# Probabilities of three slots in eight turned by a transposing DMA; q and k written and read in two steps

## Chip, core and metric

One core of a Trainium2 chip runs the kernel. The metric is the device time of one execution in microseconds. Engines are TensorE (PE, with PEld for its weight loads), VectorE (DVE), ScalarE (ACT), GpSimd (POOL) and the DMA queues, which SP, ACT and POOL issue.

## What is computed

```python
xn = layernorm(x)                                  # x: 8 x 512 x 256
qkv = (xn @ qkv_w.T).reshape(8, 512, 3, H=16, D=64)
q, k = rope(q), rope(k)
scores = einsum('bhqd,bhkd->bhqk', q, k) / 8
kb = -p * log1p(a * |i - j|)                       # p, a: one number a head
attn = softmax(scores + kb)
att = einsum('bhqk,bhkd->bhqd', attn, v) -> @ out_w.T
out = x + att + ffn(xn)                            # ffn: top-1 routing over 16 experts
```

Between q, k and the output, each head of each batch has 512 x 512 probabilities. They are made with queries on the partitions and are wanted, for the product with v, with keys on the partitions: they have to be turned, in blocks of 128 x 128.

## The kernel before

`prepare` and `experts` run first (layer norm, routing, weights, the 16 experts). They are not touched. `attention` is the rest, and the change lies in it alone.

**Slots and groups.** The attention is cut into 256 slots, 32 for each of 8 batches. Slot s takes one *pair*: two of the four 128-row query blocks of one head, 2 x 128 queries by 512 keys. Eight slots make a group, that is four heads of one batch; there are 32 groups. Each of the engines has its own hand-written program, and they are held together by semaphores alone. What stands in each engine's slot s:

- PE (`slot` at its end of the file): scores of s into `ps_s[0]` and `ps_s[1]` (four matmuls, L1296 and L1297; it waits until the scores of s-1 have been read, `negated`); a *fill*, one piece of other work in the single bank `ps_x` (q or k of the group after next in slots 0 to 3 of the group, v in slots 4 and 5, the output projection y of the group before in 6 and 7; it waits for `x_free`); eight transposes of pair s-1 into `ps_t` (L1307); the values, 24 matmuls of pair s-2 (L1323).
- DVE: `neg` of s (L1207, once for each of the two query blocks: scaled scores plus bias, negated, with the row minimum); the read of a v or y fill; `pair_lo` of s-1 (L1172), which subtracts the f16 high part of the turned probabilities from `ps_t`; in every fourth slot `read_context` ahead of neg, in the next `context_lo` at the end (L1193).
- ACT: the read of a q, k or v fill; `pair_hi` of s-1 (L1087), the f16 high part out of `ps_t`; the two exponentials of s (L1111), out of `neg` into `prob`.
- POOL: `step`, the rotation of q and k of one group (L998 to L1002) and their split into high and low f16 parts `parts` (L1008, L1012); then the gathers and sums of the expert outputs.
- SP: `turn_context`, a transposing DMA of the context's f16 parts into `ot` (L958); `move`, which writes `parts` to DRAM in four DMAs (L945), waits for them, and reads them back as `qk` and `kswap` in three (L949, L951).

All operands of large matmuls are f16 pairs, high and low part, so a product takes three matmuls (`PARTS`). Buffers `prob`, `pt`, `ps_t` and `neg` are double, by the slot's parity; `ps_s` has one bank for each query block.

## Time and profile before

| | us |
|---|---|
| median of 3 runs | 1342.48 (1341.34 to 1347.08) |
| profiled execution, device time | 1339.31 |
| its span | 1337.5 |
| attention, from its first scores to the end | about 359 to 1337 |
| one group of eight slots in the middle | 30.09 |

The page's second section shows the stages: up to about 340 us preparation and experts, with changing loads on all engines; from there an even pattern, in which PE is in nines, DVE in eights, ACT in sevens and eights. The engines' spans overlap, so a busy share tells only where to look. Which engine holds the others up is read from the waits, and what a slot costs from the chain of work in order of time: there, each piece is the time from one instruction's release to the next one's. Matmul records overlap, so their mean durations (193 ns for 64 columns) are not their cost; the chain's pieces are.

### The profile page before, as it was taken

The numbers are of one execution on the slowest core, as the hardware profiler recorded it, in microseconds if no ns is written. First come the engines' busy times: TensorE is split into PE (matmuls) and PEld (weight loads), VectorE is DVE, ScalarE is ACT, GpSimd is POOL, SyncE is SP. The second block draws the span as 40 slices with busy tenths as digits, with TensorE's granted clock in tenths as the row PEclk, the third lists the DMA queues.
The fourth block names the chain that finished last, engine by engine and source line by source line (L and its number), as shares of the span: only waits on it lengthen the run. The fifth ranks groups of instructions, "written<-read, shape, count | busy, mean of one in ns | idle before, by whom it ended". The sixth has DMA issues, their size and how long they took to land.

```text
span 1337.5 us, 33943 instructions
## 1 busy us (share of the span) xinstructions
PE 1216.2 (91%) x13412; PEld 938.0 (70%) x13412; DVE 1098.9 (82%) x2166; ACT 985.9 (74%) x1831; POOL 798.0 (60%) x628
## 2 busy tenths in 40 slices
PE   5630999997699999999999999999999999999995
PEld 5620788895267777777777777777777777777764
DVE  7864799994388888888888888888888888888894
ACT  2775688882388777777778777877778777877773
POOL 3044000001788887886788788877778887886600
PEclk9975899998899999999999999999999999999998
DMA  8625666661445444444553454355445444444411
GB/s 267 237 62 187 219 236 234 234 212 40 117 123 141 104 111 127 120 117 115 147 154 98 112 151 104 96 141 142 117 130 146 105 112 127 120 118 113 135 41 48
DMA packets 172685, 182.47 MB, mean 136 GB/s; under 512 B 78066, under 2 KB 150783, under 8 KB 172528
## 3 DMA queue, kind: packets, MB, share of 16 engines
q1 hardware_dynamic: 160256, 160.03, 41.9%
q0 software_dynamic: 4352, 12.41, 2.7%
q10 hardware_dynamic: 7920, 7.87, 2.0%
q8 instruction: 106, 1.74, 0.5%
q14 instruction: 51, 0.42, 0.1%
HBM read 109.12 MB, written 54.56 MB: 122 GB/s over the span
## 4 chain that ended last, share of the span: by engine, by line
PE 71%; ACT 1%; DMA 1%; issue 1%; DVE 1%; SPq 0%; ACTq 0%; DVEq 0%
PE ps_t L1307 17%; PE ps_o L1323 13%; PE ps_x L1263 13%; PE ps_s L1296 8%; PE ps_s L1297 8%; PE ps_x L1283 7%; PE ps_x L1273 6%; ACT prob L1111 1%; DMA kswap<-qk_dram 0%; DMA qk_dram<-parts 0%; DMA ot<-ctx_parts 0%; ACT proj L1073 0%; ACT prob L1073 0%; DVE ctx_parts L1193 0%; ACT pt_hi L1087 0%
## 5 line engine op out<-in xcount | busy, mean ns | idle before, releaser
L1172 DVE SCALAR_TENSOR_TENSOR pt_lo<-ps_t,pt_hi 128x1024 f16<-128x1024 f32 x256 | 312.6, 1221 | 129.1 <-ACT pt_hi L1087 129.1
L1207 DVE CUSTOM_DVE_ANT_0 neg<-ps_s,strips,score_scale 128x512 f32<-128x512 f32 x512 | 361.7, 743 | 8.1 <-PE ps_s L1297 8.0
L1111 ACT ACTIVATE prob<-neg,neg_max 128x512 f32<-128x512 f32 x512 | 362.6, 712 | 0.0
L1087 ACT ACTIVATE pt_hi<-ps_t 128x1024 f16<-128x1024 f32 x256 | 261.9, 1023 | 128.5 <-PE ps_t L1307 126.5
L1307 PE MATMUL ps_t<-ident,prob 128*128 128x128 f32 x2048 | 269.4, 273 | 4.3 <-ACT prob L1111 4.2
L1307 PEld LDWEIGHTS ps_t<-ident,prob 128*128 128x128 f32 x2048 | 234.3, 141 | 39.1 <-issue 10.6
L1323 PE MATMUL ps_o<-val_hi,pt_hi 128*128 128x64 f16 x2048 | 206.0, 193 | 1.8 <-DVE pt_lo L1172 1.7
L1323 PE MATMUL ps_o<-val_hi,pt_lo 128*128 128x64 f16 x2048 | 206.2, 193 | 0.0
L1323 PE MATMUL ps_o<-val_lo,pt_hi 128*128 128x64 f16 x2048 | 206.2, 193 | 0.0
L1296 PE MATMUL ps_s<-qk 128*128 128x512 f16 x512 | 195.4, 382 | 6.0 <-DMA kswap<-qk_dram 5.6
L1297 PE MATMUL ps_s<-kswap,qk 128*128 128x512 f16 x512 | 194.9, 381 | 0.0
L1323 PEld LDWEIGHTS ps_o<-val_hi,pt_hi 128*128 128x128 f16 x2048 | 184.4, 98 | 2.6 <-DVE pt_lo L1172 1.8
L1323 PEld LDWEIGHTS ps_o<-val_lo,pt_hi 128*128 128x128 f16 x2048 | 181.7, 98 | 2.9
L1323 PEld LDWEIGHTS ps_o<-val_hi,pt_lo 128*128 128x128 f16 x2048 | 181.9, 98 | 0.0
L998 POOL TENSOR_TENSOR rot<-proj,cos 128x512 f32<-128x512 f32 x62 | 78.7, 1269 | 164.5 <-ACT proj L1073 151.6
L1002 POOL TENSOR_TENSOR rot<-rot,prod 128x512 f32<-128x512 f32 x124 | 168.1, 1355 | 9.7
L1263 PE MATMUL ps_x<-xcur,wqkv_hi 128*128 128x512 f16 x512 | 154.2, 383 | 10.9 <-PEq L533 6.1
L1012 POOL TENSOR_TENSOR parts<-rot,parts 128x1024 f16<-128x1024 f32 x62 | 132.5, 2138 | 4.8
L624 POOL DMA_DIRECT2D expert_dram<-xa x16 | 11.5, 721 | 177.2 <-ACT xa L665 177.2
L1073 ACT COPY proj<-ps_x 128x512 f32<-128x512 f32 x124 | 73.0, 589 | 49.3 <-PE ps_x L1263 49.3
L1283 PE MATMUL ps_x<-wout_hi,ot 128*128 128x256 f16 x512 | 97.1, 278 | 7.0 <-DMA ot<-ctx_parts 6.1
L1263 PEld LDWEIGHTS ps_x<-xcur,wqkv_hi 128*128 128x128 f16 x512 | 49.8, 99 | 74.6 <-issue 8.5
(186 smaller groups left out, 2565.0 us busy)
## 6 DMA issues: line engine op xcount, KB each, us to landing
raw<-in_L_ffn_w_dram SPq DMA_DIRECT2D x32, 1024.0 KB, 5.1
qk_dram<-parts SPq DMA_DIRECT2D x128, 256.0 KB
qk<-qk_dram SPq DMA_DIRECT2D x32, 1024.0 KB, 5.6
kswap<-qk_dram SPq DMA_DIRECT2D x64, 256.0 KB, 6.5
xa<-in_L_attn_x_dram SPq DMA_DIRECT2D x8, 512.0 KB, 6.4
xt_dram<-xth SPq DMA_DIRECT2D x8, 512.0 KB, 5.1
slots_dram<-zeros SPq DMA_DIRECT2D x4, 1024.0 KB, 8.3
xa<-slots_dram SPq DMA_DIRECT2D x16, 256.0 KB, 5.3
```

The costliest lines, as they stand in the source:

```text
L1002: nc.gpsimd.tensor_tensor(rot[:, w, half, :], rot[:, w, half, :], prod[:], op).then_inc(turned_parts, 1)
L1012: nc.gpsimd.tensor_tensor(parts[:, w, 1], rot[:, w], parts[:, w, 0], ALU.subtract).then_inc(parts_lo, 1)
L1087: nc.scalar.activation(pt[0][:, (l - 1) % 2].rearrange("p q k c -> p q (k c)"), ps_t[l % 2][:], ACT.Copy, scale=P_SCALE).then_inc(turned_h ...
L1111: nc.scalar.activation(prob[:, l % 2, q, :], neg[:, l % 2, q, :], ACT.Exp, bias=neg_max[:, 2 * (l % 2) + q:2 * (l % 2) + q + 1], scale=-1. ...
L1172: nc.vector.scalar_tensor_tensor(out=pt[1][:, (l - 1) % 2].rearrange("p q k c -> p q (k c)"), in0=ps_t[l % 2][:], scalar=P_SCALE, in1=pt[0 ...
L1207: nc.vector.tensor_tensor_reduce(neg[:, l % 2, q, :], ps_s[q][:], strips[:, h, start:start + S], score_scale[:, 0:1], 3.0e38, ALU.add, ALU ...
L1263: last = nc.tensor.matmul(ps_x[:], wt[a][:, kt, c:c + P], xcur[:, x, kt, :], start=(m == 0), stop=(m == 3 * KT - 1))
L1283: last = nc.tensor.matmul(ps_x[:, i * M:(i + 1) * M], ot[:, x, kt, t:t + P], wot[a][:, 2 * g + kt, :], start=(m == 0), stop=(m == 5))
L1296: nc.tensor.matmul(ps_s[q][:], qk[:, j % 2, 0, k // 2, t:t + P], qk[:, j % 2, 1, k // 2, :], start=True, stop=False)
L1297: nc.tensor.matmul(ps_s[q][:], qk[:, j % 2, 0, k // 2, t:t + P], kswap[:, j % 2, k // 2, :], start=False, stop=True).then_inc(scored, 1)
L1307: last = nc.tensor.transpose(ps_t[l % 2][:, q, kt * P:(kt + 1) * P], prob[:, (l - 1) % 2, q, kt * P:(kt + 1) * P], ident[:])
L1323: last = nc.tensor.matmul(ps_o[:, c:c + D], pt[x][:, l % 2, q, kt, :], val[a][:, l2 // 8 % 4, kt, hd:hd + D], start=(m == 0), stop=(m == 3 ...
```

## The change

In slots 1, 4 and 7 of each group (`DMA_TURNS`, 95 of the 256 pairs, since the last pair stays with PE) the pair isn't transposed by PE. ACT makes the f16 high part of the unturned probabilities behind the exponentials (`prob_high`), DVE the low part at the head of its next slot (`prob_low`), both into a single buffer `prob_parts`, and SP turns both parts with one DMA straight into `pt` (`turn_probs`). PE's values wait for that DMA. `pt` is now one tile with the parts inside.

SP's `move` is cut in two: `move_out` writes q and k at a group's end, `move_in` reads them in the next group, behind the turn of the last pair. `rot` has room for q or k only, so the high and low parts of q are made before k is rotated.

```diff
 EARLY_SCATTERS = 24
+DMA_TURNS = (1, 4, 7)
 FILLS = 6
...
-        rot = sb("rot", [P, 2, 2, S])
+        rot = sb("rot", [P, 2, S])
...
-        pt = [sb(f"pt_{n}", [P, 2, 2, TPB, P], F16) for n in ("hi", "lo")]
+        pt = sb("pt", [P, 2, 2, 2, TPB, P], F16)
+        prob_parts = sb("prob_parts", [P, 2, 2, S], F16)
...
             return n
-        def pairs_turned(b, l):
-            return PAIRS * b + l
+        def by_dma(s):
+            return s % 8 in DMA_TURNS and s < NB * PAIRS - 1
+        def dma_slots(s):
+            return sum(by_dma(i) for i in range(s))
+        def pe_slots(s):
+            return s - dma_slots(s)
         def y_fills(b, j):
...
         @block.sync
         def _(sp):
-            def move(n, r):
+            def move_out(n, r):
                 F = 2 * n + r
-                wait(sp, scored, 16 * (F - 1))
                 sp.wait_ge(parts_lo, 2 * F + 2)
                 for h in range(HG):
                     sp.dma_start(qk_dram[r, :, :, :, :, h, :].rearrange("w a f d s -> d (w a f) s"),
                                  parts[32 * h:32 * h + 32].rearrange("p w a f s -> p (w a f) s")).then_inc(parts_written, 16)
+            def move_in(n, r):
+                F = 2 * n + r
+                wait(sp, scored, 16 * (F - 1))
                 sp.wait_ge(parts_written, 64 * F + 64)
                 rows = qk_dram[r].rearrange("w a f d h s -> (a f d) w (h s)")
                 sp.dma_start(qk[:, r].rearrange("p w h s -> p w (h s)"), rows).then_inc(qk_moved[r], 16)
                 for c in (0, 64):
                     sp.dma_start(kswap[64 - c:128 - c, r].rearrange("p h s -> p (h s)"), rows[c:c + 64, 1]).then_inc(qk_moved[r], 16)
+            def turn_probs(s):
+                n = dma_slots(s)
+                wait(sp, pv_done, s - 1)
+                sp.wait_ge(prob_lo, n + 1)
+                sp.dma_start_transpose(pt[:, s % 2].rearrange("p a q k c -> p (a q k) c"),
+                                       prob_parts[:].rearrange("p a q s -> p (a q s)")).then_inc(turned_by_dma, 16)
             def turn_context(b, j):
...
                 sp.dma_start(source[:], source_dram[b]).then_inc(routes_loaded, 16)
                 sp.dma_start(gate[:], gate_dram[b]).then_inc(routes_loaded, 16)
-            def batch(b):
+            def group(b, j):
+                first = PAIRS * b + 8 * j
+                if first and by_dma(first - 1):
+                    turn_probs(first - 1)
+                if first + 8 < NB * PAIRS:
+                    move_in((4 * b + j + 1) // 2, (j + 1) % 2)
+                for k in range(7):
+                    if by_dma(first + k):
+                        turn_probs(first + k)
+                    if k == 1 and first:
+                        turn_context(*divmod(4 * b + j - 1, 4))
+                    if k == 1 and j == 1 and not is_last(b):
+                        load_routes(b + 1)
+                if ahead(b, j):
+                    move_out(*ahead(b, j)[:2])
+                if j == 1 and not is_last(b):
+                    sp.wait_ge(filled, fills_before(b, 14))
+                    load_x(b + 1)
+            load_routes(0)
+            move_out(0, 0)
+            move_in(0, 0)
+            move_out(0, 1)
+            for b in range(NB):
                 for j in range(4):
-                    if j or not is_first(b):
-                        turn_context(b, j - 1)
-                    if j == 1 and not is_last(b):
-                        load_routes(b + 1)
-                        sp.wait_ge(filled, fills_before(b, 14))
-                        load_x(b + 1)
-                    if ahead(b, j):
-                        move(*ahead(b, j)[:2])
-            load_routes(0)
-            move(0, 0)
-            move(0, 1)
-            over_batches(batch)
+                    group(b, j)
             turn_context(NB - 1, 3)
             sp.wait_ge(x_free, fills_before(NB - 1, PAIRS) + 2)
...
                 for half, (first, second, op) in enumerate(((cos, sin, ALU.subtract), (sin, cos, ALU.add))):
-                    nc.gpsimd.tensor_tensor(rot[:, w, half, :], proj[:, w, 0, :], first[:], ALU.mult).then_inc(turned_parts, 1)
+                    nc.gpsimd.tensor_tensor(rot[:, half, :], proj[:, w, 0, :], first[:], ALU.mult).then_inc(turned_parts, 1)
...
             def high(F, w):
-                nc.gpsimd.tensor_copy(parts[:, w, 0], rot[:, w]).then_inc(parts_hi, 1)
+                nc.gpsimd.tensor_copy(parts[:, w, 0], rot[:]).then_inc(parts_hi, 1)
             def low(F, w):
-                nc.gpsimd.tensor_tensor(parts[:, w, 1], rot[:, w], parts[:, w, 0], ALU.subtract).then_inc(parts_lo, 1)
+                nc.gpsimd.tensor_tensor(parts[:, w, 1], rot[:], parts[:, w, 0], ALU.subtract).then_inc(parts_lo, 1)
             def step(F, fills):
                 for w in range(2):
                     rotate(F, w, fills + 2 * w + 2)
-                for w in range(2):
                     if F > 1:
                         high(F, w)
...
             def pair_hi(b, l):
-                act.wait_ge(turned, pairs_turned(b, l))
-                wait(act, pv_done, PAIRS * b + l - 2)
-                nc.scalar.activation(pt[0][:, (l - 1) % 2].rearrange("p q k c -> p q (k c)"), ps_t[l % 2][:],
+                s = PAIRS * b + l - 1
+                act.wait_ge(turned, pe_slots(s) + 1)
+                wait(act, pv_done, s - 1)
+                nc.scalar.activation(pt[:, s % 2, 0].rearrange("p q k c -> p q (k c)"), ps_t[l % 2][:],
                                      ACT.Copy, scale=P_SCALE).then_inc(turned_hi, 1)
+            def prob_high(s):
+                n = dma_slots(s)
+                act.wait_ge(exp_done, 2 * s + 2)
+                wait(act, turned_by_dma, 16 * n)
+                nc.scalar.activation(prob_parts[:, 0], prob[:, s % 2], ACT.Copy, scale=P_SCALE).then_inc(prob_hi, 1)
             def context_hi(b, l):
...
+                if s and not by_dma(s - 1):
                     pair_hi(b, l)
                 for q in range(2):
                     act.wait_ge(negated, 2 * s + q + 1)
-                    if q == 0:
-                        wait(act, turned, pairs_turned(b, l - 1))
+                    if q == 0 and s >= 2:
+                        if by_dma(s - 2):
+                            act.wait_ge(prob_lo, dma_slots(s - 1))
+                        else:
+                            act.wait_ge(turned, pe_slots(s - 1))
                     nc.scalar.activation(prob[:, l % 2, q, :], neg[:, l % 2, q, :], ACT.Exp,
                                          bias=neg_max[:, 2 * (l % 2) + q:2 * (l % 2) + q + 1], scale=-1.0,
                                          accum_out=sums[:, l // 4 % 2, 2 * (l % 4) + q:2 * (l % 4) + q + 1]).then_inc(exp_done, 1)
+                if by_dma(s):
+                    prob_high(s)
                 if l % 4 == 2 and not (is_first(b) and l == 2):
                     context_hi(b, l)
...
             def pair_lo(b, l):
-                dve.wait_ge(turned_hi, pairs_turned(b, l))
-                nc.vector.scalar_tensor_tensor(out=pt[1][:, (l - 1) % 2].rearrange("p q k c -> p q (k c)"), in0=ps_t[l % 2][:],
-                                               scalar=P_SCALE, in1=pt[0][:, (l - 1) % 2].rearrange("p q k c -> p q (k c)"),
+                s = PAIRS * b + l - 1
+                dve.wait_ge(turned_hi, pe_slots(s) + 1)
+                nc.vector.scalar_tensor_tensor(out=pt[:, s % 2, 1].rearrange("p q k c -> p q (k c)"), in0=ps_t[l % 2][:],
+                                               scalar=P_SCALE, in1=pt[:, s % 2, 0].rearrange("p q k c -> p q (k c)"),
                                                op0=ALU.mult, op1=ALU.subtract).then_inc(turned_lo, 1)
+            def prob_low(s):
+                dve.wait_ge(prob_hi, dma_slots(s) + 1)
+                nc.vector.scalar_tensor_tensor(out=prob_parts[:, 1], in0=prob[:, s % 2], scalar=P_SCALE, in1=prob_parts[:, 0],
+                                               op0=ALU.mult, op1=ALU.subtract).then_inc(prob_lo, 1)
             def read_context(b, l):
...
                 h = HG * j + k // 2
+                if s and by_dma(s - 1):
+                    prob_low(s - 1)
                 if l % 4 == 2 and not (is_first(b) and l == 2):
                     read_context(b, l)
...
                 kind = slot_kind(b, l)
                 if kind:
                     read_fill(kind, b, l, fills_before(b, l))
-                if l or not is_first(b):
+                if s and not by_dma(s - 1):
...
                 dve.wait_ge(x_free, 2 * w + 2)
                 if w:
-                    dve.wait_ge(turned_parts, 6)
+                    dve.wait_ge(parts_lo, 1)
...
             for w in range(2):
+                turn_first(w)
                 dve.wait_ge(parts_hi, w + 1)
-                nc.vector.tensor_tensor(parts[:, w, 1], rot[:, w], parts[:, w, 0], ALU.subtract).then_inc(parts_lo, 1)
+                nc.vector.tensor_tensor(parts[:, w, 1], rot[:], parts[:, w, 0], ALU.subtract).then_inc(parts_lo, 1)
...
                 s = PAIRS * b + l
-                wait(pe, turned_lo, pairs_turned(b, l - 2))
+                wait(pe, turned_lo, pe_slots(s - 2))
...
+                s = PAIRS * b + l2
+                if by_dma(s):
+                    pe.wait_ge(turned_by_dma, 16 * (dma_slots(s) + 1))
+                else:
+                    pe.wait_ge(turned_lo, pe_slots(s) + 1)
                 for q in range(2):
...
-                            last = nc.tensor.matmul(ps_o[:, c:c + D], pt[x][:, l % 2, q, kt, :],
+                            last = nc.tensor.matmul(ps_o[:, c:c + D], pt[:, s % 2, x, q, kt, :],
                                                     val[a][:, l2 // 8 % 4, kt, hd:hd + D], start=(m == 0), stop=(m == 3 * TPB - 1))
                             m += 1
...
                     fill(kind, b, l, fills_before(b, l))
-                if l or not is_first(b):
+                s = PAIRS * b + l
+                if s and not by_dma(s - 1):
                     transposes(b, l)
```

What the diff does to the order, first on DVE, slots 1 and 2 of a group: `neg` is the reduction of the scores, `ctxt` the read of the context. Before:

```order
L1207 ISA neg,neg_max<-ps_s0,strips,score_scale 128x512
L1207 ISA neg_max 128x1
L1207 ISA neg,neg_max<-ps_s1,strips,score_scale 128x512
L1207 ISA neg_max 128x1
L1172 SCALAR_TENSOR_TENSOR pt_lo<-ps_t1,pt_hi 128x1024
L1181 RECIPROCAL rsum<-sums 128x8
L1183 TENSOR_TENSOR ctxt<-ps_o,rsum 128x2x4x64
L1207 ISA neg,neg_max<-ps_s0,strips,score_scale 128x512
L1207 ISA neg_max 128x1
L1207 ISA neg,neg_max<-ps_s1,strips,score_scale 128x512
L1207 ISA neg_max 128x1
L1172 SCALAR_TENSOR_TENSOR pt_lo<-ps_t0,pt_hi 128x1024
```

and in the changed kernel:

```order
L1260 ISA neg,neg_max<-ps_s0,strips,score_scale 128x512
L1260 ISA neg_max 128x1
L1260 ISA neg,neg_max<-ps_s1,strips,score_scale 128x512
L1260 ISA neg_max 128x1
L1218 SCALAR_TENSOR_TENSOR pt<-ps_t1,pt 128x1024
L1224 SCALAR_TENSOR_TENSOR prob_parts<-prob,prob_parts 128x1024
L1232 RECIPROCAL rsum<-sums 128x8
L1234 TENSOR_TENSOR ctxt<-ps_o,rsum 128x2x4x64
L1260 ISA neg,neg_max<-ps_s0,strips,score_scale 128x512
L1260 ISA neg_max 128x1
L1260 ISA neg,neg_max<-ps_s1,strips,score_scale 128x512
L1260 ISA neg_max 128x1
```

The low part of pair 1 used to be made at the end of slot 2, after both neg; it now stands at the head of slot 2, before the context is read and before both neg, and reads `prob`.

ACT, from the exponentials of a group's slot 7 to the read of the q fill in slot 2 of the next, with the semaphores that each instruction waits for. Before:

```order
L1111 ACTIVATE prob,sums<-neg,neg_max 128x512 [waits turned,negated]
L1111 ACTIVATE prob,sums<-neg,neg_max 128x512 [waits negated]
L1073 COPY proj<-ps_x 128x512 [waits rotations,filled]
L1087 ACTIVATE pt_hi<-ps_t 128x1024 [waits pv_done,turned]
L1111 ACTIVATE prob,sums<-neg,neg_max 128x512 [waits turned,negated]
L1111 ACTIVATE prob,sums<-neg,neg_max 128x512 [waits negated]
L1073 COPY proj<-ps_x 128x512 [waits rotations,filled]
L1087 ACTIVATE pt_hi<-ps_t 128x1024 [waits pv_done,turned]
L1111 ACTIVATE prob,sums<-neg,neg_max 128x512 [waits turned,negated]
L1111 ACTIVATE prob,sums<-neg,neg_max 128x512 [waits negated]
L1073 COPY proj<-ps_x 128x512 [waits rotations,filled]
```

and in the changed kernel:

```order
L1154 ACTIVATE prob,sums<-neg,neg_max 128x512 [waits turned,negated]
L1154 ACTIVATE prob,sums<-neg,neg_max 128x512 [waits negated]
L1128 ACTIVATE prob_parts<-prob 128x1024 [waits turned_by_dma,exp_done]
L1106 COPY proj<-ps_x 128x512 [waits rotations,filled]
L1154 ACTIVATE prob,sums<-neg,neg_max 128x512 [waits turned,negated]
L1154 ACTIVATE prob,sums<-neg,neg_max 128x512 [waits negated]
L1106 COPY proj<-ps_x 128x512 [waits rotations,filled]
L1121 ACTIVATE pt<-ps_t 128x1024 [waits pv_done,turned]
L1154 ACTIVATE prob,sums<-neg,neg_max 128x512 [waits prob_lo,negated]
L1154 ACTIVATE prob,sums<-neg,neg_max 128x512 [waits negated]
L1128 ACTIVATE prob_parts<-prob 128x1024 [waits turned_by_dma,exp_done]
L1106 COPY proj<-ps_x 128x512 [waits rotations,filled]
```

The eviction of pair 7 out of `ps_t`, which stood in slot 0 ahead of that slot's exponentials, has gone; `prob_parts` is written behind the exponentials of slots 7 and 1, ahead of the read of the next slot's fill. Pair 0 is evicted in slot 1 as before.

SP, a little over one group. Before:

```order
L945 DMA qk_dram<-parts 32x8x512 x4
L949 DMA qk<-qk_dram 128x2x2048
L951 DMA kswap<-qk_dram 64x2048 x2
L958 DMA_TRANSPOSE ot<-ctx_parts 128x16x128
L945 DMA qk_dram<-parts 32x8x512 x4
L949 DMA qk<-qk_dram 128x2x2048
L951 DMA kswap<-qk_dram 64x2048 x2
```

and in the changed kernel:

```order
L955 DMA qk_dram<-parts 32x8x512 x4
L973 DMA_TRANSPOSE pt<-prob_parts 128x16x128
L964 DMA qk<-qk_dram 128x2x2048
L966 DMA kswap<-qk_dram 64x2048 x2
L973 DMA_TRANSPOSE pt<-prob_parts 128x16x128
L981 DMA_TRANSPOSE ot<-ctx_parts 128x16x128
L973 DMA_TRANSPOSE pt<-prob_parts 128x16x128
L955 DMA qk_dram<-parts 32x8x512 x4
L973 DMA_TRANSPOSE pt<-prob_parts 128x16x128
```

The context's DMA (`ot`) now has the turn of pair 1 ahead of it and that of pair 4 behind it; the four writes stand between the turns of pair 4 and pair 7, and the reads behind that of pair 7.

## Rows read from the trace of the kernel before

**Rows 1.** the page, section 1: busy us (share of the span) xinstructions of each engine
```profile
PE 1216.2 (91%) x13412; PEld 938.0 (70%) x13412; DVE 1098.9 (82%) x2166; ACT 985.9 (74%) x1831; POOL 798.0 (60%) x628
```

**Rows 2.** windows: busy us (xinstructions) of each engine, PEclk the granted clock, DMA share
```profile
600.00:800.00 200.00, 200.00 (x2389) 150.09 (x2385) 171.64 (x331) 159.82 (x321) 154.17 (x117) 1.00 0.49 130
...
1200.00:1310.00 110.00, 107.17 (x1302) 77.33 (x1300) 97.39 (x190) 86.13 (x175) 46.06 (x35) 1.00 0.37 97
```

**Rows 3.** waits, 420 to 1310 us: who waited for whom, us in total, times, longest
```profile
ACT pt_hi L1087 <- PE ps_t L1307: 118.2, 232, 1.3
```

**Rows 4.** chain in order of time, attention: start us, us, engine, tile, line
```profile
601.11 1.29 PE ps_x L1263 x6
602.41 0.87 PE ps_t L1307 x8
604.84 1.29 PE ps_x L1263 x6
...
607.01 0.70 PE ps_o L1323 x24
...
623.63 1.31 PE ps_x L1283 x12
...
627.37 1.39 PE ps_x L1283 x12
...
631.20 1.29 PE ps_x L1263 x6
```

**Rows 5.** timeline, ACT, one slot: start us, us, instruction, [idle before <-releaser]
```profile
603.32 1.02 ACT L1087 ACTIVATE pt_hi<-ps_t 128x1024 f16<-128x1024 f32 x1 [0.29 <-PE ps_t L1307]
604.24 0.71 ACT L1111 ACTIVATE prob<-neg,neg_max 128x512 f32<-128x512 f32 x1
...
605.55 0.19 ACT L1111 ACTIVATION_READ_ACCUMULATOR prob<-neg,neg_max 128x1 f32 x1
```

**Rows 6.** timeline, DVE, one slot and a v fill's read
```profile
608.11 1.22 DVE L1172 SCALAR_TENSOR_TENSOR pt_lo<-ps_t,pt_hi 128x1024 f16<-128x1024 f32 x1 [1.17 <-ACT pt_hi L1087]
609.25 0.19 DVE L1181 RECIPROCAL rsum<-sums 128x8 f32<-128x8 f32 x1
...
610.08 0.74 DVE L1207 CUSTOM_DVE_ANT_0 neg<-ps_s,strips,score_scale 128x512 f32<-128x512 f32 x1
...
611.42 0.08 DVE L1207 DVE_READ_ACCUMULATOR2_ANT neg_max<- 128x1 f32 x1
...
618.97 0.68 DVE L1157 TENSOR_TENSOR val_lo<-ps_x,val_hi 128x512 f16<-128x512 f32 x1
```

**Rows 7.** timeline, start-up of attention: DVE and ACT split q and k
```profile
339.19 1.23 DVE L1233 TENSOR_TENSOR parts<-rot,parts 128x1024 f16<-128x1024 f32 x1 [1.41 <-ACT parts L1082]
343.49 2.03 DVE L1233 TENSOR_TENSOR parts<-rot,parts 128x1024 f16<-128x1024 f32 x1 [3.07 <-ACT parts L1082]
...
342.40 1.05 ACT L1082 CAST parts<-rot 128x1024 f16<-128x1024 f32 x1
```

**Rows 8.** instructions on tile ot: its transposing DMA, 32 of them, to landing
```profile
DMA to landing us min/median/max: 3.6/3.7/5.4
```

**Rows 9.** chain in order of time, the end of the kernel
```profile
1323.42 3.66 DMA ot<-ctx_parts
```

**Rows 10.** instructions of two DVE lines: duration ns min/median/max, first and last start
```profile
L1172 DVE SCALAR_TENSOR_TENSOR pt_lo<-ps_t,pt_hi x256: 1204/1224/1226, 368.8 to 1318.8; 128x1024 f16<-128x1024 f32 x128
...
L1193 DVE SCALAR_TENSOR_TENSOR ctx_parts<-ctxt,ctx_parts x64: 681/682/1618, 390.7 to 1322.7; 128x512 f16<-128x512 f32 x64
```

**Rows 11.** timeline, POOL: first and last instruction on q and k of one group
```profile
606.84 1.27 POOL L998 TENSOR_TENSOR rot<-proj,cos 128x512 f32<-128x512 f32 x1 [5.52 <-ACT proj L1073]
...
626.91 2.13 POOL L1012 TENSOR_TENSOR parts<-rot,parts 128x1024 f16<-128x1024 f32 x1
```

**Rows 12.** chain in order of time, last two groups, no q, k, v fills
```profile
1281.06 0.22 PE ps_s L1296
...
1307.70 0.22 PE ps_s L1296
```

More of the change, by code:

```diff
@@ L995, in rotate @@
                 wait(pool, turned_parts, done)
-                wait(pool, parts_lo, 2 * F - 1 + w)
+                wait(pool, parts_lo, 2 * F + w)
                 for half, (first, second, op) in enumerate(((cos, sin, ALU.subtract), (sin, cos, ALU.add))):
-                    nc.gpsimd.tensor_tensor(rot[:, w, half, :], proj[:, w, 0, :], first[:], ALU.mult).then_inc(turned_parts, 1)
+                    nc.gpsimd.tensor_tensor(rot[:, half, :], proj[:, w, 0, :], first[:], ALU.mult).then_inc(turned_parts, 1)
                     wait(pool, turned_parts, done + 3 * half)
@@ L1001, in rotate @@
                     pool.wait_ge(turned_parts, done + 3 * half + 2)
-                    nc.gpsimd.tensor_tensor(rot[:, w, half, :], rot[:, w, half, :], prod[:], op).then_inc(turned_parts, 1)
+                    nc.gpsimd.tensor_tensor(rot[:, half, :], rot[:, half, :], prod[:], op).then_inc(turned_parts, 1)
             def high(F, w):
```

11 lines of the change are left out of this document (4 added, 7 removed).

## Prediction

> **What bounds the kernel now.** I read the page first: PE is busy for 1216 us, 91% of the span, and no other engine for more than 82% [rows 1]. The windows of the attention stage say more: between 600 and 800 us PE is busy for all of 200 us, DVE for 172, ACT for 160, POOL for 154, and the granted clock is 1.00 [rows 2]. The waits agree: between 420 and 1310 us ACT waits 118 us for PE's transposes [rows 3]. So PE's own work sets the pace. The chain in order of time shows what a slot costs: six fill matmuls 1.29, eight transposes 0.87, 24 value matmuls 0.70, and the rest, up to 3.73 us, the four score matmuls. The same place of two groups (eight slots each) is 30.09 us apart [rows 4]. There are 32 groups, of which the first 30 make q, k and v for a later group.
>
> **What is removed.** 95 of 256 pairs of probability tiles no longer take eight transposes on PE. At 0.87 us [rows 4] that is 83 us of PE's work. Counted alone it gives 1342.5 - 83 = 1259.6 us. ACT's and DVE's two instructions for the pair don't go away: they now split the untransposed tile, 128x1024 elements from SBUF. An ACT cast of just that shape from SBUF takes 1.05 us, against 1.02 for the eviction now; a DVE subtraction of that shape with two SBUF inputs takes 1.23, against 1.22 [rows 5, 6, 7]. In time spent, the two engines gain and lose nothing.
>
> **What is moved, and why it matters.** Now the pair's split comes after the transposes, one slot behind, while DVE already works on the next scores. In the changed order prob_high(s) stands behind both exponentials of s on ACT, and prob_low(s) stands at the head of DVE's slot s+1, ahead of the two reductions that make neg(s+1). Behind that wait are queued: neg(s+1), for which ACT's exponentials of s+1 wait, and for which PE's scores of s+2 wait (they need the banks ps_s), then PE's fill of s+2, transposes of s+1 and values of s, in that order. So a turned slot ties ACT, DVE and PE into one chain without overlap. I price it from X, the end of the transposes of s-1, to the end of the transposes of s+1:
> - ACT's eviction of s-1 starts 0.04 after X and lets the next start 0.92 later: 0.96. Two exponentials up to the end of the accumulator read, 604.24 to 605.74: 1.50. prob_high 1.05, and 0.05 for the two handovers: 3.56 [rows 5, 7].
> - prob_low, start to next start: 1.14, as from 608.11 to 609.25. So 4.70.
> - neg(s+1), both halves and the last read, 610.08 to 611.50: 1.42 [rows 6]. So 6.12.
> - PE's second scores 0.04 + 0.43, fill 1.29, transposes 0.87: 2.63 [rows 4]. So 8.75.
> This is the price for s = 7. For s = 1 DVE reads the context ahead of neg(2), 609.25 to 610.08, 0.83 more: 9.58. For s = 4 the fill of slot 6 must wait for DVE's read of the v fill: it starts 1.34 after neg(5) did, takes 0.68, and 0.04 to PE; the fill takes 1.31 to 1.39: 4.70 + 1.34 + 0.72 + 1.35 + 0.87 = 8.98 [rows 4, 6]. Between two chains stands a plain step of PE (values, scores, fill, transposes), 3.75 and 3.79; between 7 and the next 1 there is none, since the transposes that end chain 7 (those of slot 8) are those from which the next chain 1 starts.
> Period of a group: 9.58 + 3.75 + 8.98 + 3.79 + 8.75 = 34.85 us, against 30.09: **4.8 us slower**, though PE has 2.6 us less to do.
>
> **The DMA transpose.** It moves 512 KB, exactly what the context's transpose moves. That one takes 3.6 to 5.4 us from issue to landing, median 3.7 [rows 8], and 3.66 at the end where nothing else runs [rows 9]. Issued at X + 4.75 to 4.80, it lands at X + 8.5, and the values that need it stand behind the transposes that end at X + 8.75, 8.98 or 9.58. So it is just covered and I take nothing. If every one took 5.4 it would land at 10.2: 1.4 + 1.2 + 0.6 = 3.2 us per group on top, which is the upper bound. SP has nothing else to issue then.
> The Trainium skill (VectorE: DVE Perf Modes, The three transpose paths) gives 390 ns for a 128x128 tile on TensorE and 1309 ns by DMA. That is for single tiles: by it 16 tiles one after another would take 21 us by DMA, and the row of 3.7 us for 16 tiles speaks against using it so; the sum goes by the row.
>
> **The port of DVE and POOL.** pt_lo reads PSUM and one SBUF tile, and all 256 lie between 1.204 and 1.226 us. prob_low has two SBUF inputs. The instruction of that kind on ctx_parts takes 0.681 at the least and 1.618 at the most, and the 128x1024 one took 1.23 us once and 2.03 once, with POOL at work [rows 7, 10]. POOL rotates and splits q and k from 606.84 to 629.04 in a group [rows 11]. In the new period chain 7's prob_low falls behind POOL's last instruction, and I take 0; chains 1 and 4 fall inside its rotations, where it may wait for an instruction of 1.27 us. Chain 1 keeps step with the rotations (both start from the same fill); I take 0.2 for it and half an instruction, 0.65, for chain 4. Bounds 0 and 2.5 us a group. Sum 0.85: period 35.7, **5.6 us over before**.
> The Trainium skill (SBUF — State Buffer, SBUF: two separate sides) says of this that a DVE instruction with two SBUF inputs and a GpSimd one that reads SBUF exclude each other for a whole instruction. The trace agrees, with 2.03 beside 1.23. By that rule the wait can reach a whole POOL instruction, which is the upper bound already taken.
>
> **q and k in two steps.** The write to DRAM now stands at the end of a group on SP, ahead of the turn of pair 7, and waits for POOL. The read stands behind that turn, a group later. POOL's parts end 22.2 us after its start at 606.84 [rows 11]; with two blocked instructions and a start some 0.2 us before chain 1's X it ends about 24 to 25 us after that X, and the turn of pair 7 is wanted at 3.75 + 3.79 + 9.6 + 9.0 + 4.8 + 0.8 = 31.7. Four writes take about 3 us to issue. No wait; 0 us. The q and k themselves have 20 us of slack. In the start-up the single rot tile makes DVE's second rotation wait for the first low part (ready at 339.19 + 1.23), so the second low part can't end before about 347.5 instead of 345.5, and ACT's last high part waits for POOL longer: 2 to 6 us once, I take 4 [rows 7].
>
> **The last two groups** have no q, k or v fills: 26.6 us a group before (1281.06 to 1307.70) [rows 12]. The chains barely shorten, because the exponential of s+1 takes the fill's place: about 33.7. So +7, and +6 for the last, whose pair 7 isn't turned by DMA.
>
> **Sum.** 30 x 5.6 + 7 + 6 + 4 = 185 us. The profiled execution is 1339.3 us (span 1337.5), the median 1342.5, 0.24% more. 1339.3 + 185 = 1524; on the median 1527. I take 1526 us.
>
> **The rivals.**
> 1. *PE keeps setting the pace (faster).* If the ACT and DVE handovers ran ahead of PE, so that neg(s+1) were ready when PE reached slot s+2, only the 83 us would count: about 1262 us. For it: PE is busy 100% and DVE only 86%. It decides at a chain of 3.75 + 2.86 = 6.6 us from X (two slots, one without transposes); mine has 8.75 or more. Against it: every link is a wait in the order below, with a duration from a row. The chance is that I misread one. 5%.
> 2. *The transposing DMA is the end of the chain.* If in company (writes of q and k, their 1 MB read issued right behind it) it takes 5.4 us, the period is 3.2 us longer: about 1526 + 96 = 1622 us. For it: two transposes a group come near the q and k traffic. Against it: the median of 32 is 3.7 amid the same traffic. 8%.
> 3. *SP's queue.* If POOL were slowed to end after 31.7, each late microsecond delays pair 7's turn by as much. At 3 us a group: about 1620 us. 4%.
> 4. *Chains and POOL balance to no change:* the price would have to fall from 185 to under 7 us. 1%.
> The forecast has 82%. PE's clock is no case for me: in the stage of 1200 to 1310, where PE waits in each slot of the last groups, it was granted 1.00 [rows 2].
>
> **How the numbers follow.** Without any port wait the sum is 30 x 4.8 + 13 + 2 = 159, thus 1501; with 2.5 us of it per group 30 x 7.3 + 13 + 6 = 238, thus 1580. Links may be 0.1 us off, three chains a group: 10 us either way. Range 1483 to 1592. A measurement of this kernel tells 0.5% (7 us) from no change. Faster 5%, within 0.5% 1%, slower 94%.
>
> **What would show it.** Right: PE busy about 82% in the middle of attention; waits of PE's scores on DVE's neg_max of 2 us in slots 3, 6 and 9; DVE idle ahead of prob_low, released by ACT; groups 35 to 36 us apart; prob_low with a minimum near 1.22 and some at 2. Wrong: PE waiting longest for the DMA into pt (rival 2), SP's writes late (rival 3), or PE at 100% (rival 1).

## The result, and the profile after

The changed kernel takes 1613.61 us (median of 4 runs, 1603.6 to 1617.76) against 1343.16 us: a ratio of 1.2043 [1.1992, 1.2094]. I had forecast 1526 us, range 1483 to 1592. It is slower, as forecast, but by 270 us and not by 185: the time lies above my range.

The page's busy times of the changed kernel, and the windows of two stages (columns as in [rows 1] and [rows 2]):

```profile
PE 1259.0 (78%) x12652; PEld 887.8 (55%) x12652; DVE 1134.8 (70%) x2166; ACT 996.1 (62%) x1831; POOL 857.8 (53%) x628
```

```profile
600.00:800.00 200.00, 161.25 (x1689) 105.38 (x1686) 139.50 (x254) 123.97 (x246) 135.62 (x95) 0.91 0.53 135
1200.00:1310.00 110.00, 88.73 (x899) 58.20 (x897) 71.64 (x134) 64.96 (x131) 70.19 (x50) 0.88 0.52 132
```

PE has 760 matmuls fewer and is busy 43 us longer than in [rows 1]. The column behind the busy times (PEclk, the share of TensorE's clock that was granted) goes with it: it was 1.00 in both stages before [rows 2] and is 0.91 and 0.88 now. Every engine has a smaller share than before: nobody is the bound, they wait for each other. The waits from 450 to 1500 us (columns as in [rows 3]):

```profile
PEld ps_s L1348 <- DVE neg_max L1260: 142.1, 160, 2.7
ACT prob L1154 <- DVE neg_max L1260: 138.5, 76, 3.4
...
PE ps_o L1379 <- DVE ctxt L1234: 81.0, 28, 3.9
DVE prob_parts L1224 <- ACT prob_parts L1128: 67.7, 82, 1.3
...
PE ps_x L1315 <- DMA xcur<-xt_dram: 21.1, 6, 4.3
...
PE ps_o L1379 <- DMA pt<-prob_parts: 0.3, 1, 0.3
```

Lines one, two and four are the chain that I forecast: DVE's low part behind ACT's high part, and PE's scores and ACT's exponentials behind DVE's neg. The last line says that the new DMA almost never ends a wait. Lines three and five I had not foreseen. Here is the chain in order of time through slots 1 and 2 of a clean group, to be read against [rows 4]:

```profile
943.03 0.89 PE ps_t L1359 x8
...
944.86 1.52 ACT prob L1154 x4
...
946.41 1.06 ACT prob_parts L1128
...
947.50 1.23 DVE prob_parts L1224
...
948.87 0.70 DVE ctxt L1234
...
949.61 0.94 PE ps_o L1379 x24
950.55 0.43 PE ps_s L1348
...
952.26 2.07 PE ps_x L1315 x6
954.33 0.87 PE ps_t L1359 x8
```

From X (943.92) to the end of the last transposes (955.20) it is 11.28 us; I had 9.58. The links of ACT and DVE are mine. What is new: the way goes through the context's read to PE's *values*, since these overwrite the bank `ps_o` that DVE has just read, and then through four scores of 0.43 and six fill matmuls of 2.07 that took 0.22 and 1.29 before [rows 4, 12]. PE had waited until 949.61 for the context (28 such waits, 2.9 us on average), and its clock was then at its lower level (1.2 GHz) from 950.3 to 953.7.

Below, the *period* is the distance between the first exponentials of two groups, and a *split* is such a distance between two slots. Before: 30.1 us. After: 37.0 in clean groups, the others up to 42.4; sum over the first 31 periods 1190.4 us against 926.6. The clock's records have the lower level for 184 us of this stretch, and for none of it before.

### The profile page after: what moved, and what is told of

Read it like the earlier page. It is cut to its first block, busy times and chain, and to the rows that moved or that the text cites. A ratio compares the mean times of both kernels' runs of the same rounds, so it can differ in the third digit from the quotient of the medians.

```text
span 1612.2 us, 32518 instructions
## 1 busy us (share of the span) xinstructions
PE 1259.0 (78%) x12652; PEld 887.8 (55%) x12652; DVE 1134.8 (70%) x2166; ACT 996.1 (62%) x1831; POOL 857.8 (53%) x628
## 4 chain that ended last, share of the span: by engine, by line
PE 36%; ACT 14%; DVE 10%; issue 10%; POOL 5%; DMA 4%; SPq 1%; DVEq 0%; ACTq 0%; POOLq 0%
PE ps_t L1359 8%; PE ps_x L1315 8%; ACT prob L1154 8%; ACT prob_parts L1128 5%; PE ps_x L1335 5%; PE ps_o L1379 5%; PE ps_s L1348 5%; DVE neg L1260 4%; PE ps_s L1349 4%; DVE prob_parts L1224 3%; DMA xcur<-xt_dram 2%; PE ps_x L1325 2%; POOL rot L1036 1%; DMA pt<-prob_parts 1%; POOL rot L1032 1%
## 5 line engine op out<-in xcount | busy, mean ns | idle before, releaser
L1218 DVE SCALAR_TENSOR_TENSOR pt<-ps_t,pt 128x1024 f16<-128x1024 f32 x161 | 196.7, 1222 | 234.2 <-ACT pt L1121 233.1
L1379 PE MATMUL ps_o<-val_hi,pt 128*128 128x64 f16 x4096 | 234.9, 197 | 98.1 <-DVE ctxt L1234 91.6
L1379 PEld LDWEIGHTS ps_o<-val_hi,pt 128*128 128x128 f16 x4096 | 217.2, 101 | 122.3 <-DVE ctxt L1234 106.8
L1121 ACT ACTIVATE pt<-ps_t 128x1024 f16<-128x1024 f32 x161 | 165.0, 1025 | 140.7 <-PE ps_t L1359 140.7
L1379 PE MATMUL ps_o<-val_lo,pt 128*128 128x64 f16 x2048 | 218.5, 197 | 0.0
L1379 PEld LDWEIGHTS ps_o<-val_lo,pt 128*128 128x128 f16 x2048 | 189.4, 101 | 6.7 <-issue 1.8
L1224 DVE SCALAR_TENSOR_TENSOR prob_parts<-prob,prob_parts 128x1024 f16<-128x1024 f32 x95 | 123.9, 1304 | 80.2 <-ACT prob_parts L1128 80.2
L1359 PE MATMUL ps_t<-ident,prob 128*128 128x128 f32 x1288 | 175.7, 281 | 1.3 <-ACT prob L1154 1.2
L1359 PEld LDWEIGHTS ps_t<-ident,prob 128*128 128x128 f32 x1288 | 156.1, 147 | 20.7 <-issue 8.5
L1046 POOL TENSOR_TENSOR parts<-rot,parts 128x1024 f16<-128x1024 f32 x62 | 132.4, 2135 | 10.2 <-ACT parts L1115 5.3
L1315 PE MATMUL ps_x<-xcur,wqkv_lo 128*128 128x512 f16 x256 | 109.1, 426 | 0.0
```

Of the source, the lines that this page charges most:

```text
L1121: nc.scalar.activation(pt[:, s % 2, 0].rearrange("p q k c -> p q (k c)"), ps_t[l % 2][:], ACT.Copy, scale=P_SCALE).then_inc(turned_hi, 1)
L1218: nc.vector.scalar_tensor_tensor(out=pt[:, s % 2, 1].rearrange("p q k c -> p q (k c)"), in0=ps_t[l % 2][:], scalar=P_SCALE, in1=pt[:, s % ...
L1224: nc.vector.scalar_tensor_tensor(out=prob_parts[:, 1], in0=prob[:, s % 2], scalar=P_SCALE, in1=prob_parts[:, 0], op0=ALU.mult, op1=ALU.sub ...
L1315: last = nc.tensor.matmul(ps_x[:], wt[a][:, kt, c:c + P], xcur[:, x, kt, :], start=(m == 0), stop=(m == 3 * KT - 1))
L1359: last = nc.tensor.transpose(ps_t[l % 2][:, q, kt * P:(kt + 1) * P], prob[:, (l - 1) % 2, q, kt * P:(kt + 1) * P], ident[:])
L1379: last = nc.tensor.matmul(ps_o[:, c:c + D], pt[:, s % 2, x, q, kt, :], val[a][:, l2 // 8 % 4, kt, hd:hd + D], start=(m == 0), stop=(m == 3 ...
```

## The experiments

In each, the change is to the changed kernel unless another is named; ratios are to the kernel before.

**1. The context's read ahead of the low part.** Is the chain's longest piece the read of the context behind `prob_low`?

```diff
-                if s and by_dma(s - 1):
-                    prob_low(s - 1)
                 if l % 4 == 2 and not (is_first(b) and l == 2):
                     read_context(b, l)
+                if s and by_dma(s - 1):
+                    prob_low(s - 1)
```

> The changed kernel with one move on DVE: in slot 2 of a group the context is read ahead of the low part of pair 1, not behind it. In the changed kernel PE stands at its values of slot 2 until the context is read (81 us in 28 waits), idle for up to 3.9 us, and the score and value matmuls behind that idle time then take twice as long each (0.43 us where 0.22 is usual, 1.46 for 24 where 0.70 is usual). Theory (idle time brings the clock down): without that wait PE's idle stretch shrinks to some 1.9 us, its matmuls keep their short durations, chain 1 falls from 11.3 us to the 9.0 of the other two, 2.3 us a group, 74 us in all: about 1540 us, granted clock of the attention up from 0.93 to near 1. Rival (the context's read costs its own time only): 0.8 us a group, about 1587 us, clock as before.

1608.92 us, 1.1994 [1.1933, 1.2055]: no expectation held. In groups of 37.0 us of both kernels, the split from slot 1 to 2 fell from 5.40 to 4.56, but the next is 6.0 to 6.1 where it was 5.9, the one of slot 4 went from 4.6 to 5.2, and the lower clock is still there in each group, now after PE's wait for neg_max. Taking away one wait only hands it to the next. What PE did ahead of such a fall, in the group at 941 us (the first two rows are a timeline, columns as in [rows 5]; the last a window):

```profile
947.47 0.20 PE L1379 MATMUL ps_o<-val_hi,pt 128*128 128x64 f16 x1 [0.35 <-DVE ctxt L1234]
...
949.80 0.39 PE L1348 MATMUL ps_s<-qk 128*128 128x512 f16 x1 [1.46 <-DVE neg_max L1260]
...
951.00:954.00 3.00, 3.00 (x9) 1.16 (x7) 0.96 (x4) 0.82 (x3) 2.77 (x4) 0.50 0.52 117
```

Here the clock fell behind two waits of 0.35 and 1.46 us with 24 value matmuls between them; 12 of the 29 falls between 450 and 1300 us had no wait above 1.5 us in the 6 us ahead of them.

**2. The low part at the end of DVE's slot**, behind neg and the fill's read, so that neg isn't held up.

```diff
-                if s and by_dma(s - 1):
-                    prob_low(s - 1)
...
                     pair_lo(b, l)
+                if s and by_dma(s - 1):
+                    prob_low(s - 1)
```

> The changed kernel with the low part of a DMA-turned pair moved on DVE from the head of the slot to its end, behind both reductions of the scores and the read of the fill, where the low part of the other pairs stands. Theory (the order on DVE ties three engines into one chain): the reductions and exponentials of the next slot no longer wait for the split, the DMA lands 8.5 us after the last transposes and becomes the end of what PE waits for, a group takes 31 to 32 us instead of 37: about 1400 us (1380 to 1430). Rival (the transposing DMA itself, or its company, is what costs): a group stays above 35 us, over 1550 us.

1691.66 us, 1.2644 [1.2557, 1.2731]: I was wrong by far. The waits name what took the chain's place:

```profile
PE ps_o L1379 <- DMA pt<-prob_parts: 223.9, 77, 6.7
```

The low part, and with it the transfer, now comes at least the 1.42 us of neg later, and nothing covers it. So the DMA was covered only because the chain was long; experiment 6, the same order without the DMAs and with x early, is 344 us shorter.

**3. x early:** on SP, the load of the next x ahead of the four writes of q and k.

```diff
-                if ahead(b, j):
-                    move_out(*ahead(b, j)[:2])
                 if j == 1 and not is_last(b):
                     sp.wait_ge(filled, fills_before(b, 14))
                     load_x(b + 1)
+                if ahead(b, j):
+                    move_out(*ahead(b, j)[:2])
```

> The changed kernel with the load of the next batch's x issued ahead of the writes of q and k on SP instead of behind them. In the changed kernel PE waits for it six times in 1050 us, 21 us in all, up to 4.3 us, and each such wait is followed by a stretch of half clock. Theory: the writes' wait for POOL and their own transfer delay the load: all seven waits go, 25 to 40 us less, about 1580 us. Rival (the load is slow by itself): no change.

1600.73 us, 1.1925 [1.1846, 1.2004]. No wait for x is left; 13 us, about half of the least that I expected, and the intervals of the two ratios overlap a little. Counted from the first exponentials of each profiled execution it is 22.6 us (see below).

**4. No transposing DMA.** The 95 DMAs are left out, and PE multiplies zeros in their place, so this part of the computation is missing; the waits are those for the low part.

```diff
-                sp.dma_start_transpose(pt[:, s % 2].rearrange("p a q k c -> p (a q k) c"),
-                                       prob_parts[:].rearrange("p a q s -> p (a q s)")).then_inc(turned_by_dma, 16)
...
-                wait(act, turned_by_dma, 16 * n)
+                wait(act, prob_lo, n)
...
                 if by_dma(s):
-                    pe.wait_ge(turned_by_dma, 16 * (dma_slots(s) + 1))
+                    pe.wait_ge(prob_lo, dma_slots(s) + 1)
```

> The changed kernel without the 95 transposing DMAs of the probabilities (this part of the computation is left out): the split into prob_parts stays, and PE's values of these pairs wait for the low part only. Theory (the DMA is covered by the chain of ACT, DVE and PE): within 5 us of the changed kernel's 1614, unless the DMAs' traffic is what makes the load of x late, then up to 30 less. Rival of the prediction (the DMA is the end of the chain, 3.2 us a group): about 1510.

1610.91 us, 1.2036 [1.1968, 1.2104]: the same time, within 3 us, without the transfers. In the changed kernel they cost nothing that can be told from noise.

**5. The two steps alone:** no pair is turned by DMA, all else as changed.

```diff
-DMA_TURNS = (1, 4, 7)
+DMA_TURNS = ()
```

> The changed kernel with no slot turned by DMA (all 256 pairs with PE as before): what is left of the change is q and k written and read in two steps, the single rot tile, and the later issue of the load of x. Theory: this part costs only the start-up (2 to 6 us) and a few microseconds for each late x, so 1345 to 1375; all the rest comes from the turned slots.

1424.78 us, 1.0599 [1.0554, 1.0644]: a clear miss. The part that I had priced at 4 us costs 82. Every fourth group takes 38.5 to 40.0 us; the chain in order of time of one of them:

```profile
686.89 2.15 POOL parts L1046
...
689.06 0.32 SPq L955
...
689.42 0.45 SPq L955
...
689.91 0.73 SPq L955
...
691.03 0.93 SPq L955
...
692.01 5.54 DMA xcur<-xt_dram
...
697.60 2.74 PE ps_x L1315 x6
```

x is wanted by the first q fill of a batch. Its load now stands behind the four writes, and these wait for POOL's last low part. POOL ends, the writes are issued in 2.9 us, x lands 5.5 later, and PE, after that wait, needs 2.74 for the fill that takes 1.29.

**6. As 2, with x early and without the DMAs** (the same part of the computation is left out as in 4).

> The order of e2 (low part behind the reductions) with x loaded early, and without the transposing DMAs of the probabilities (left out; PE's values wait for the low part only). e2 was 1692 us, and PE waited 360 us for the DMA into pt. Theory (with the split out of the chain of ACT, DVE and PE, only the DMA's 3.7 us and what the idle time does to the clock hold PE up): this one falls to 1300 to 1370, a group 28 to 31 us. Rival (ACT's and DVE's order alone keeps a group at 35 us or more, whatever the DMA does): over 1480.

1347.65 us, 1.0033 [1.0002, 1.0064], period 29.7 to 30.8, as expected. With the split off the chain and transfers that cost nothing, 83 us less of PE's work still gain nothing. What sets the pace here isn't shown: between 600 and 800 us PE is busy for 190 us at a clock of 1.00, DVE for 179, POOL for 171 and ACT for 158, and the chain of a group still passes through PE, ACT and DVE in turn. The result bounds what this change could have brought in this order of work.

**7. PE kept busy.** As 3, and PE turns the identity matrix 16 times in the slots in which it has no pair to turn, into a half of `ps_t` that is free then.

```diff
+            def keep_awake(s, l):
+                wait(pe, turned_lo, pe_slots(s - 2))
+                for i in range(16):
+                    nc.tensor.transpose(ps_t[l % 2][:, 0, 0:P], ident[:], ident[:])
...
                     transposes(b, l)
+                elif s:
+                    keep_awake(s, l)
```

> The kernel of e3 (x early, 1601 us) with work added: in each slot in which PE has no pair to transpose it turns the identity 16 times into the idle half of ps_t, 1.75 us of PE time, where it would wait for DVE anyway. Theory (a group of 37.0 us is a chain of 35.3 us at full clock, and the rest is half clock behind PE's waits): PE has no long idle stretch, the granted clock goes to near 1, a group takes 35.3 us or a little more, 1530 to 1550 us. Rival (the clock is a symptom, not a cost, or PE's time is what counts): no change, or 95 x 1.75 = 166 us slower.

1552.43 us, 1.1564 [1.1508, 1.1621], just above the band: PE is given 95 x 16 transposes of no use, 95 times the 1.75 us of the last row below, 166 us, and the kernel is 48 us *faster* than in 3. Windows, and the chain through slots 1 and 2:

```profile
600.00:800.00 200.00, 186.45 (x2121) 138.14 (x2118) 151.79 (x279) 132.46 (x264) 148.49 (x104) 1.00 0.59 141
```

```profile
1110.08 1.52 ACT prob L1154 x4
...
1111.62 1.07 ACT prob_parts L1128
...
1112.71 1.23 DVE prob_parts L1224
...
1114.08 0.70 DVE ctxt L1234
...
1114.83 0.87 PE ps_o L1384 x24
...
1116.77 1.29 PE ps_x L1315 x6
1118.07 0.89 PE ps_t L1359 x8
...
1126.44 1.75 PE ps_t L1366 x16
```

The clock is 1.00, the fill 1.29 again, the chain from X (1109.13) to 1118.95 is 9.82, and clean groups take 35.8 us: the period that I had forecast, 35.7. As the last row shows, the useless transposes themselves lie on the chain in one place, slot 5. The other groups take 37.0 or more. In the one at 883 us the chain has the transfer in it, which there is no longer covered; the second fence has these waits from 450 to 1500 us:

```profile
891.58 5.86 DMA pt<-prob_parts
```

```profile
PE ps_o L1384 <- DMA pt<-prob_parts: 17.0, 19, 2.3
```

**8. Two pairs, values one slot later:** pairs 1 and 4, low part late as in 2, x early, the values of a turned pair one slot later on PE.

> A version that should not tie the engines: pairs 1 and 4 of a group only are turned by DMA, the low part is made behind the reductions, x is loaded early, and the values of a DMA-turned pair are computed one slot later, together with those of the next pair, so that the DMA has 3.7 us more. Theory: the DMA lands 9.7 us after the last transposes and is wanted at 9.6; no wait of more than some tenths; PE has 1.75 us less to do in a group of 30.1. About 28.8 us a group, 1311 us (1290 to 1345), under the kernel before. Rival (any hand-over of a pair to ACT, DVE and DMA costs more than PE's 0.87 us): over 1345.

1405.68 us, 1.0481 [1.0436, 1.0527]: a miss. There are two `pt` buffers, and the eviction of a later pair now waits for the late values, which is the largest new wait (450 to 1300 us); that it makes up the whole miss was argued from this row only:

```profile
ACT pt L1121 <- PE ps_o L1378: 96.5, 54, 3.9
```

A third buffer would take 4096 bytes more of each partition; no run has one.

**9 to 11. The parts added one by one**, all with x early: no pair, pair 4 alone, pair 1 alone (`DMA_TURNS` is `()`, `(4,)`, `(1,)`).

> No pair is turned by DMA; q and k move in two steps; the load of the next x stands ahead of the four writes of q and k on SP. Theory (the 82 us of the two steps alone are seven late x loads, with the half clock behind them, plus 0.7 us in each group where POOL's low part of q now meets DVE's subtraction on ctx_parts): the x waits go, 30.8 us a group everywhere, so 1343 + 30 x 0.7 + about 8 at the start = 1372 us, range 1360 to 1385. Rival (the groups of 38 to 40 us have another cause, such as the order of the reads on SP): above 1400 us, with waits of PE's fill that another DMA ends.

> As the run without turned pairs and with the early x, but pair 4 of each eight is turned by DMA. Theory (each turned pair puts one chain in the place of two ordinary slots, and the chains add up): chain 4 took 9.26 us in the changed kernel, two slots take 7.6, so 1.7 us a group on 30.8, thus 32.5: 1343 + 30 x 2.4 + 10 = 1425 us. Rival (the first wait of PE brings its half clock with it whatever the number of turned pairs, 1.7 us a group more): 34.2 us a group, about 1475 us.

> As before, with pair 1 of each eight turned instead of pair 4. Theory (chains add up, and a single wait of PE leaves its clock alone): 9.58 against 7.5 us, 2.1 us a group on 30.8, thus 32.9: 1343 + 30 x 2.8 + 10 = 1437 us. Rival (PE's wait for the values of the slot behind, up to 3.9 us in the changed kernel, is by itself what lets the clock fall): 1.7 us more a group, 34.6 us, about 1488 us, and the granted clock of the attention stage under 1.00.

| kernel | us | ratio | period | lower clock in a group |
|---|---|---|---|---|
| no pair | 1371.78 | 1.0203 [1.0154, 1.0252] | 30.8 | none |
| pair 4 | 1407.61 | 1.0479 [1.0429, 1.0529] | 31.8 | none |
| pair 1 | 1481.39 | 1.1020 [1.0965, 1.1075] | 34.4 | 3.4 us |

The first is as expected: 53 of the 82 us were x. What is left of it in the middle of attention is 0.7 us a group, all in the split of slot 4 (4.52 against 3.84). The timeline (columns as in [rows 5]) shows POOL, then DVE:

```profile
603.36 2.14 POOL L1046 TENSOR_TENSOR parts<-rot,parts 128x1024 f16<-128x1024 f32 x1
```

```profile
604.36 1.69 DVE L1244 SCALAR_TENSOR_TENSOR ctx_parts<-ctxt,ctx_parts 128x512 f16<-128x512 f32 x1
```

q's low part is now made in the middle of a group and meets DVE's subtraction on the context, which takes 0.68 alone [rows 10] and here ends 0.55 behind POOL's end at 605.50. The Trainium skill (SBUF — State Buffer, SBUF: two separate sides) has the later one of such two fully blocked until the first is done; the trace agrees within 0.13 us.

Pair 4 came out 17 us under my 1425: I had added its chain on top of the 0.7, but both lie in the split of slot 4. Pair 1 went by the rival: one wait of PE in a group, here for the context's read, is enough for the clock. Windows and waits (450 to 1300 us), first of pair 4, then of pair 1:

```profile
600.00:800.00 200.00, 189.44 (x2217) 137.76 (x2216) 168.89 (x314) 151.84 (x304) 155.20 (x114) 1.00 0.50 131
```

```profile
PE ps_s L1348 <- DVE neg_max L1260: 41.6, 54, 1.4
```

```profile
600.00:800.00 200.00, 181.99 (x2080) 132.35 (x2076) 157.13 (x295) 141.65 (x283) 147.51 (x108) 0.95 0.47 122
```

```profile
PE ps_o L1379 <- DVE ctxt L1234: 71.2, 25, 2.9
```

Waits of up to 1.4 us, one of 1.3 and one of 0.2 in each group, left the clock at 1.00; 25 waits of 2.8 us on average, one in each group, did not. Between these two kernels both the longest wait and the sum of the waits grow, so they don't tell which of the two counts.

**12. A version made from these:** pairs 0, 2 and 5, the low part right behind neg, the values of a turned pair a slot later and ahead of the transposes, x early; on SP the context's DMA stands one slot later, behind the turn of pair 2.

> A version made from what the runs before showed. Pairs 0, 2 and 5 of each eight are turned by DMA; DVE takes prob_low behind neg of the next slot and not ahead of it; the values of such a pair stand one slot later on PE, ahead of the transposes; x is loaded ahead of the writes. Theory (with the split off the chain and the DMA given a slot more, DVE and ACT set the pace as in the run without the transfers, 29.7 to 30.8 us a group): 1345 to 1375 us. Rival 1 (PE's saved 2.6 us a group count): about 1290 us. Rival 2 (with two pt buffers ACT waits for the values of the slot before, as in the run of pairs 1 and 4): above 1400 us.

1555.31 us, 1.1547 [1.1475, 1.162]: a miss. Two waits for the transfer take over (450 to 1500 us, in the longest of the four executions, 1564.25 us):

```profile
PE ps_o L1378 <- DMA pt<-prob_parts: 98.5, 29, 6.2
ACT prob_parts L1128 <- DMA pt<-prob_parts: 93.1, 29, 6.1
```

The second one is the single buffer `prob_parts`: the high part of the next turned pair can't be written before the last transfer has landed. Which of the two comes first wasn't separated. No version of the change beat the kernel before.

## Why the prediction failed where it did

**What held.** PE's 83 us don't count; a turned slot ties ACT, DVE and PE into one chain. At full clock a clean group came out as priced: 35.8 measured in experiment 7, 35.7 predicted. In splits: 30.8 (no pair, experiment 9), 2.36 more for chain 1 (5.39 + 4.43 against 7.46, experiment 7), 1.06 for chain 4 (the period of experiment 10 less that of 9) and 1.52 for chain 7 (8.98 against 7.46, experiment 7) make 35.7. Two of the three additions come from the run that the sum is compared with, so this shows no more than that chain 4 costs about the same alone and in company. Part of it is luck: chains 1, 4 and 7 were 0.24, 0.5 and 0.23 longer than the links that I had summed (the middle one by the collision at `ctx_parts`), and the 0.85 that I had set apart for port waits of `prob_low` covered that. `prob_low` itself hardly waits for POOL:

```profile
L1224 DVE SCALAR_TENSOR_TENSOR prob_parts<-prob,prob_parts x95: 1224/1226/2699, 373.4 to 1577.7; 128x1024 f16<-128x1024 f32 x95
```

Its mean is 1.30, so 0.08 an instruction and 0.2 a group. The collision that counted was the one at `ctx_parts`. That `prob_low` waits little holds for this order only: in experiment 6, where `prob_low` stands later in the slot, its mean was 1.59. The DMA being covered held as well (experiment 4).

**Where the other 88 us are.** In differences of runs:

1. *"PE's clock is no case for me"*: this step failed; 48 us (experiment 3 less 7), by far the largest. I had read the clock from [rows 2], the stage of 1200 to 1310, in which PE is busy for 107 of 110 us in spite of its waits. That showed a clock of 1.00 with few and short waits; PE's only row of that stage of the kernel before has 10 of them, 0.3 us at most:

```profile
PE ps_t L1307 <- ACT prob L1111: 2.7, 10, 0.3
```

It said nothing on a PE that waits 2 us and more in one piece, as my own chain had it. What the runs showed in its place: the clock fell in each group, 184 us of lower clock in 31 periods, and the links behind the falls took longer (four scores 0.43 for 0.22 us each, a fill 2.07 for 1.29). The row I should have made is how long PE waits, not in how many slots.

2. *"q and k in two steps ... No wait; 0 us"*: failed. I asked when the writes were wanted by the turn of pair 7, and left out what else stands behind them on SP: the load of x. 13 us in the changed kernel (after less experiment 3), 53 where nothing else is late (5 less 9). I also had moved POOL's low part of q without asking what it would now meet: 0.7 us a group, which lies inside the 35.8.
3. *Rival 2, the DMA as the end of the chain*: true in part of the groups, but only at full clock (experiment 7: 19 waits, 17 us). The lower clock hides it in the changed kernel. So the 48 us are net of these 17. If all of the 17 is lost time, the clock by itself takes some 65: an estimate, since no run has the full clock without the uncovered transfers.
4. *The chain through slot 2*: I followed neg(2), and had overlooked that PE's values in that slot wait for the context's read behind `prob_low`. In length it is 9.82 against 9.58, but it holds the wait of 2.8 us behind which the clock fell. Without that wait the clock fell behind others (experiment 1).

48 + 13 + 17 = 78 us of 88. The other 10 weren't tested. The first group took 38.0 us, with 10 us of lower clock, 10.3 more than before where 5.6 were priced, and the last one took 9.8 more where 6 were.

These sizes are differences of whole runs, and the stretch ahead of the attention, in which the changed kernel and experiments 3 and 7 have the same program, differs by as much: the first exponentials stand at 366.7 us in the changed kernel's profiled execution, at 378.7 in experiment 3's and at 372.8 in experiment 7's, with the lower clock for 123, 161 and 140 us of it. Counted from there the late x is 22.6 us, the clock 45.6, and experiment 7 is 24.4 above the prediction. The clock stays the largest either way, and the late x comes ahead of the transfers.

Rivals 1, 3 and 4 are out: PE waits everywhere, SP's turn of pair 7 is not late, and the time isn't the same. My range failed because its ends were made of links and port waits alone, and held no case in which a known cost (a matmul's 0.22 us) changes. (By its own terms it would also have been 1491 to 1590, 10 us on either side of 1501 and 1580, and not 1483 to 1592.)

## To carry to other kernels

When an edit turns TensorE from busy to waiting, list the waits that it gets, how long each is and how close together they stand: its next matmuls may take twice as long, and adding useless work can then pay (here 166 us of it gained 48). When a blocking wait is put on a queue, list everything behind it until that queue's next wait, rare loads above all. And a transfer that is hidden behind a long chain is uncovered by each repair of that chain, so take a run of the repaired order without the transfer first (experiment 6): it tells what the repair is worth at best.

## What the runs showed of the hardware

- TensorE's clock fell behind each of 25 waits of PE of 2.8 us, one in a period of 34 us (experiment 11, granted clock 0.95), behind waits of 2.0 us in the changed kernel, and behind 0.35 and 1.46 us close together in experiment 1. Waits of up to 1.4 us, 54 of them, left it at 1.00 (experiment 10), and so did one of 2.3 us in experiment 7 (granted clock 1.00 from 450 to 1300 us) and those of up to 1.6 us in experiment 6. So in these runs the length of the longest wait doesn't decide by itself; what does wasn't separated. The row of experiment 6:

```profile
PE ps_o L1378 <- DVE ctxt L1232: 14.0, 34, 1.6
```

- The load of x lands in 5.4/5.6/8.8 us (least, median, most) and takes 1.2 us to issue behind four writes, against 3.2/3.4/8.8 and 0.32 where it stands ahead of them. Issue of the changed kernel, then of experiment 9:

```profile
L985 SPq DMA_DIRECT2D xcur<-xt_dram x7: 909/1185/1301, 435.4 to 1360.9; - x7
```

```profile
L985 SPq DMA_DIRECT2D xcur<-xt_dram x7: 319/320/320, 424.9 to 1163.3; - x7
```

- A transposing DMA of 512 KB lands in 3.7 us at the median, as [rows 8] say, also in experiment 7 (3.6/3.7/7.2) and, within 0.1 us, in experiment 12 (3.6/3.8/10.2). What the slow ones met, as that of 5.86 us in experiment 7, was not found.
